# Two-layer transformer on one core: the softmax rescale moves to GpSimd, and the attention pipeline's offsets change

## The reference

```python
def _L0_attn_ref(x, Wq, Wk, Wv):            # H, R = 8, 64; d = 128
    Q = (x @ Wq.T).reshape(b, n, H, R)
    K = (x @ Wk.T).reshape(b, n, H, R)
    V = (x @ Wv.T).reshape(b, n, H, d)
    attn = jnp.einsum('bnhr,bmhr->bhnm', Q, K)
    attn = jax.nn.softmax(attn, axis=-1)
    return jnp.einsum('bhnm,bmhd->bnd', attn, V)
...
def _L0_ffn_ref(...):                        # 8 experts, top 1, capacity 80
    ...
    dispatch = jnp.einsum('nec,nd->ecd', sec_mask, tokens)
    h = jax.nn.gelu(jnp.einsum('ecd,edf->ecf', dispatch, w1) + b1[:, None, :])
    expert_out = jnp.einsum('ecf,efd->ecd', h, w2) + b2[:, None, :]
    return jnp.einsum('nec,ecd->nd', combine_weights, expert_out)
```

## Time and profile before

| | |
|---|---|
| time, median of 3 runs | 1496.58 us (1493.58 to 1497.97) |
| the profiled execution | 1496.05 us, of which the span 1494.3 us |
| first layer's attention (first copy of activations to the last result) | 31.28 to 421.00 us |
| busy over the whole span | PE 82%, DVE 86%, ACT 78%, POOL 53% |
| chain that ended last, by line | DVE L1024 17%, PE L1304 9%, PE L1317 7%, DVE L1010 6% |

### The profile page before, as it was taken

The page is one execution under the profiler, slowest core; times in us unless marked ns, Lnnn a source line. Parts: engine busy times, 40 slices in busy tenths (PEclk is TensorE's granted clock), DMA queues, the critical chain, the costliest instruction groups (busy, mean ns, idle before and its releaser), DMA issues.

```text
span 1494.3 us, 25209 instructions
## 1 busy us (share of the span) xinstructions
PE 1229.9 (82%) x6185; PEld 575.0 (38%) x6185; DVE 1280.2 (86%) x3505; ACT 1158.9 (78%) x1324; POOL 789.9 (53%) x1166
## 2 busy tenths in 40 slices
PE   2798687878864788899888988899888998899887
PEld 1476455555541233333333333333333333333333
DVE  5686687878866689999999999999999999999997
ACT  1566576767725689998899899998899998998960
POOL 2702100000000278878788777888788877887730
PEclk7899899999977799999999999999999999999998
DMA  5002200000000000000000000000000000000001
GB/s 183 13 1 34 16 1 0 0 0 0 0 1 18 7 19 26 19 18 21 26 23 18 18 28 25 18 18 18 28 25 18 18 28 25 18 18 18 28 25 32
DMA packets 38780, 31.58 MB, mean 21 GB/s; under 512 B 6150, under 2 KB 35609, under 8 KB 38738
## 3 DMA queue, kind: packets, MB, share of 16 engines
q1 hardware_dynamic: 37714, 29.76, 6.7%
q0 software_dynamic: 1024, 1.35, 1.0%
HBM read 29.10 MB, written 2.75 MB: 21 GB/s over the span
## 4 chain that ended last, share of the span: by engine, by line
DVE 30%; PE 26%; issue 9%; DVEq 3%; ACT 1%; POOL 0%; ACTq 0%
DVE arena L1024 17%; PE ps L1304 9%; PE ps L1317 7%; DVE arena L1010 6%; PE ps L1361 4%; PE ps L1381 2%; PE ps L1353 2%; DVE x L1067 2%; PE ps L1335 2%; DVE z L1050 2%; DVE spread L1076 1%; DVE nmax L1016 1%; DVEq L1023 1%; DVEq L1067 1%; ACT arena L1161 1%
## 5 line engine op out<-in xcount | busy, mean ns | idle before, releaser
L1024 DVE SCALAR_TENSOR_TENSOR arena<-arena,ps 128x512 f32<-128x512 f32 x1024 | 663.1, 679 | 65.9 <-PE ps L1317 65.7
L1161 ACT ACTIVATE arena<-arena,eps 128x4096 f32<-128x4096 f32 x128 | 474.3, 3709 | 38.6 <-POOL arena L1284 38.1
L1317 PE MATMUL ps<-spread,sel 128*128 128x512 f16 x1024 | 348.5, 386 | 118.4 <-DVE arena L1024 112.1
L1278 POOL TENSOR_SCALAR arena<-kT,negq 128x512 f32<-128x512 f32 x480 | 331.6, 701 | 196.5 <-DVE arena L1024 181.3
L1284 POOL TENSOR_SCALAR arena<-arena,q 128x512 f32<-128x512 f32 x480 | 351.8, 743 | 22.4
L1304 PE MATMUL ps<-arena,phi_cols 128*32 128x512 f32 x2048 | 276.4, 614 | 20.2 <-ACT arena L1161 20.2
L1317 PEld LDWEIGHTS ps<-spread,sel 128*128 128x128 f16 x1024 | 92.1, 97 | 513.0 <-DVE arena L1024 438.4
L1149 ACT ACTIVATE arena<-kT,q 128x512 f32 (+1 forms) x330 | 217.8, 715 | 3.0
L489 ACT ACTIVATE kT<-ps,region 128x512 f32<-128x512 f32 x128 | 88.2, 689 | 101.3 <-DVE region L559 97.7
L1270 POOL TENSOR_SCALAR negq<-q 128x256 f32<-128x256 f32 x4 | 3.5, 870 | 297.6 <-POOLq L762 297.6
L1010 DVE TENSOR_SCALAR arena<-kT,q 128x512 f32 (+1 forms) x214 | 141.9, 686 | 0.3 <-PEq L762 0.3
(11 more groups left out here) (196 smaller groups left out, 1794.9 us busy)
## 6 DMA issues: line engine op xcount, KB each, us to landing
wge<-in_e_wg SPq DMA_DIRECT2D x32, 256.0 KB, 2.7
w1e<-in_e_w SPq DMA_DIRECT2D x32, 128.0 KB, 2.1
w2e<-in_e_w SPq DMA_DIRECT2D x32, 128.0 KB, 2.1
w3e<-in_e_w SPq DMA_DIRECT2D x32, 128.0 KB, 2.1
region<-in_w SPq DMA_DIRECT2D x1, 2048.0 KB
out<-x SPq DMA_DIRECT2D x4, 256.0 KB, 2.7
region<-in_wqk SPq DMA_DIRECT2D x1, 512.0 KB, 4.6
region<-in_wv SPq DMA_DIRECT2D x1, 512.0 KB, 5.3
```

The lines of the kernel that those rows point to most:

```text
L1024: dve.scalar_tensor_tensor(feat[:, j, k, :], feat[:, j, k, :], 1.0, psB[:, k % BANKS, :], ALU.mult, ALU.mult, accum_out=sums[:, j, gg, c:c ...
L1161: act.activation(grp, grp, ACT.Sqrt, bias=eps[:]).then_inc(e_ready, 2)
L1278: pool.tensor_scalar(feat[:, j, QUADS * gg + c, :], kT[:, b * N:(b + 1) * N], HUGE, negq[:, b % 2, at - b * N // 2:at - b * N // 2 + 1], A ...
L1317: pe.matmul(psB[:, k % BANKS, :], sel[:, gg, c, :], spread[:, j, :], start=True, stop=True).then_inc(bc_done, 1)
```

## The change

The rescale of every step goes to GpSimd, so L567 on VectorE and L496 on ScalarE disappear, with the semaphore `act_p_ready`. The offsets change: queries and keys of the next head are projected in step 0 of a head instead of 1, their high parts made in step 1 instead of 2, their low parts in step 2 instead of 3. The transposes come 3 steps behind instead of 2, `pT_lo` 4 instead of 3, and the value products 5 instead of 4. The output of the batch before is taken at step 6 instead of 5, and the drain is one step longer. GpSimd's other work is now dealt out between the rescales: three scatters first and the other 13 one behind each rescale of batch 0, one part of the constants behind each rescale from step 16 of batch 0 on, and one gather behind each rescale of steps 2 to 17 of batch 1. GpSimd's list is written out for all 128 steps.

```diff
-        ON_ACT = (2,)
-        QK_AT, QK_HI, QK_LO = 1, 2, 3
-        LAG_T, LAG_LO, LAG_W = 2, 3, 4
+        QK_AT, QK_HI, QK_LO = 0, 1, 2
+        LAG_T, LAG_LO, LAG_W = 3, 4, 5
...
-
-        OUT_AT = 5
+        SCATTERS_FIRST, CONSTANTS_AT, GATHERS_AT = 3, 16, 2
+
+        OUT_AT = 6
         DRAIN = OUT_AT + 3
...
+            def rescale(n):
+                pool.wait_ge(rden_ready, n + 1)
+                pool.tensor_scalar(ex[:, n % 4, :], ex[:, n % 4, :], 1.0, rden[:, n % 4:n % 4 + 1],
+                                   ALU.mult, ALU.mult).then_inc(p_ready, 1)
+
+            pool.wait_ge(zeroed, 1)
+            for t in range(SCATTERS_FIRST):
+                scatter(t)
+            for b in range(B):
+                for s in range(STEPS):
+                    rescale(b * STEPS + s)
+                    if b == 0 and s + SCATTERS_FIRST < NT:
+                        scatter(s + SCATTERS_FIRST)
+                    if b == 0 and s >= CONSTANTS_AT:
+                        prepare_constants(pool, g, c2_made, c2_prep, s - CONSTANTS_AT)
+                    if b == 1 and 0 <= s - GATHERS_AT < NT:
+                        gather(s - GATHERS_AT)
             pool.wait_ge(gathered_in, 16 * NT)
...
-                    late = s - 1
-                    if late % TB in ON_ACT and runs(late, first, drain):
-                        act.wait_ge(rden_ready, b * STEPS + late + 1)
-                        act.activation(ex[:, late % 4, :], ex[:, late % 4, :], ACT.Copy,
-                                       scale=rden[:, late % 4:late % 4 + 1]).then_inc(act_p_ready, 1)
...
-                        if late % TB not in ON_ACT:
-                            dve.wait_ge(rden_ready, b * STEPS + late + 1)
-                            dve.tensor_scalar(ex[:, late % 4, :], ex[:, late % 4, :], rden[:, late % 4:late % 4 + 1], None,
-                                              ALU.mult).then_inc(p_ready, 1)
...
-                            pe.wait_ge(p_ready, b * (STEPS - sum(by_act)) + late + 1 - n)
+                        pe.wait_ge(p_ready, b * STEPS + late + 1)
```

More of the change, by code:

```diff
@@ L401, in first_layer @@
         qk_done, qk_kept = sem("qk_done"), sem("qk_kept")
-        k_lo_filled, act_p_ready = sem("k_lo_filled"), sem("act_p_ready")
+        k_lo_filled = sem("k_lo_filled")
         q_hi_kept, k_hi_kept, v_hi_kept, lo_kept = (sem("q_hi_kept"), sem("k_hi_kept"), sem("v_hi_kept"),
@@ L444, in _, with scatter @@
             pool.memset(zero, 0.0).then_inc(zeroed, 1)
-            for t in range(NT):
+            def scatter(t):
                 pool.indirect_dma_start(
@@ L449, in _, with gather @@
                     g.xn[:, t, :], None, bounds_check=SLOTS - 1, oob_is_err=False).then_inc(g.scattered, 16)
-            pool.wait_ge(zeroed, 1)
-            prepare_constants(pool, g, c2_made, c2_prep)
-            pool.wait_ge(eo_out, 16)
-            for t in range(NT):
+            def gather(t):
+                if t == 0:
+                    pool.wait_ge(eo_out, 16)
                 pool.indirect_dma_start(
@@ L668, in row @@
                     if runs(late, first, drain):
-                        by_act = [k % TB in ON_ACT for k in range(STEPS)]
-                        n = sum(by_act[:late % STEPS + 1]) - (sum(by_act) if late < 0 else 0)
-                        if late % TB in ON_ACT:
-                            pe.wait_ge(act_p_ready, b * sum(by_act) + n)
-                        else:
-                            pe.wait_ge(p_ready, b * (STEPS - sum(by_act)) + late + 1 - n)
+                        pe.wait_ge(p_ready, b * STEPS + late + 1)
                         if not first or late >= 2:
@@ L727, in _, with prepare_constants @@
             row(B, drain=True)
-def prepare_constants(pool, g, made, prep):
-    pool.memset(g.sel[:], 0.0).then_inc(made, 1)
-    pool.memset(g.mask_c, 1.0).then_inc(made, 1)
-    pool.memset(g.phi_cols[:], 0.0)
-    pool.memset(g.weT[:, D:DV], 0.0)
-    pool.memset(g.V2[:, :, D:DV], 1.0)
-    pool.memset(g.sumsT[:], 0.0)
-    pool.memset(g.exT[:], 0.0)
-    pool.memset(g.eps[:], EPS_RHO)
-    pool.memset(g.rho, -math.sqrt(EPS_RHO))
-    pool.wait_ge(made, 2)
-    v = g.sel[:].rearrange("p g c (h a) -> p g c h a", h=2)
-    for gg in range(GROUPS):
+def prepare_constants(pool, g, made, prep, part):
+    v = g.sel[:].rearrange("p g c (h a) -> p g c h a", h=2)
+    if part == 0:
+        pool.memset(g.sel[:], 0.0).then_inc(made, 1)
+    elif part == 1:
+        pool.memset(g.mask_c, 1.0).then_inc(made, 1)
+        pool.memset(g.phi_cols[:], 0.0)
+        pool.memset(g.weT[:, D:DV], 0.0)
+        pool.memset(g.V2[:, :, D:DV], 1.0)
+    elif part == 2:
+        pool.memset(g.sumsT[:], 0.0)
+        pool.memset(g.exT[:], 0.0)
+        pool.memset(g.eps[:], EPS_RHO)
+        pool.memset(g.rho, -math.sqrt(EPS_RHO))
+    elif part < 3 + GROUPS:
+        gg = part - 3
+        if gg == 0:
+            pool.wait_ge(made, 2)
         for half in range(2):
@@ L751, in prepare_constants @@
                 ins.then_inc(prep, 1)
-    pool.affine_select(out=g.mask_c, in_=g.mask_c, compare_op=ALU.is_ge, fill=0.0, base=-16,
-                       pattern=[[-32, QUADS]], channel_multiplier=1).then_inc(made, 1)
-    pool.wait_ge(made, 3)
-    pool.affine_select(out=g.mask_c, in_=g.mask_c, compare_op=ALU.is_ge, fill=0.0, base=31,
-                       pattern=[[32, QUADS]], channel_multiplier=-1).then_inc(made, 1)
+    elif part == 3 + GROUPS:
+        pool.affine_select(out=g.mask_c, in_=g.mask_c, compare_op=ALU.is_ge, fill=0.0, base=-16,
+                           pattern=[[-32, QUADS]], channel_multiplier=1).then_inc(made, 1)
+    elif part == 4 + GROUPS:
+        pool.wait_ge(made, 3)
+        pool.affine_select(out=g.mask_c, in_=g.mask_c, compare_op=ALU.is_ge, fill=0.0, base=31,
+                           pattern=[[32, QUADS]], channel_multiplier=-1).then_inc(made, 1)
 def second_route(nc, g, take):
```

## The result

The changed kernel took 1505.63 us, median of 4 runs (1502.41 to 1508.69), against 1495.47 for the kernel before beside it (1493.58 to 1497.97): ratio 1.0067, 95% interval 1.004 to 1.0093. I had forecast 1486 and a gain. It is slower.

The account below looks back on a forecast made before the run. The prediction took a chain through TensorE, VectorE and ScalarE in the first layer's attention as the bound; -5.5, -10.15, 2 x 1.85 and +1.3 summed to -10.65 us, giving 1486 us, range 1478 to 1501.

Parts of the forecast that it names:

- Walked on through the batch: Sum of the new order's changes over the seam and heads of a looped batch: +1.85 us each.
- The walk: Adding start-to-start edges along the first layer's chain through the engines; 9.84 us per head before, 9.83 in the new order.
- I expect both stalls to go: Spread indirect DMAs would remove the stalls in batches 0 and 1: 6.12 us and 12.0 us less.
- Rival (b): The burst of indirect DMAs does not make the stalls, so both stay: +7.9 us, 1504 us; chance 0.15.
- Cost nothing: The rescale on GpSimd, 701 ns, is hidden by two steps of cover; at most 1 us a step otherwise.
- Batch 0, -5.5: First batch: 8.3 us less from stall, held rescale and clock, against +1.1, +2.0 and about -0.3 elsewhere.
- Heads: Heads without value projections would take 9.83 us in the new order, those with two 11.34.
- For the seam the walk had +0.8: At a batch's start, the first scores of head 1 would come 0.8 us later.
- The drain, +1.3: At the end, half a head's value products ahead of the last transposes and the last GpSimd rescale: +1.3 us.
- the second layer, taken as 0: The layer after the changed attention, left alone by the change, got no term in the sum.

Follow-up runs that it names:

- filler_light: Changed kernel plus one-pass filler matmuls in the loop, ten at a batch's seam, six ahead of the transposes of steps 7 and 15; 1500.92 us, ratio 1.0124.
- before_again: The kernel before, unchanged, profiled again beside the experiments; 1480.41 us in its one run.
- e1_spread_only: Kernel before with only GpSimd's scatters, constants and gathers paced by step, rescale still on VectorE and ScalarE; 1482.52 us, ratio 1.0005.
- e2: Changed kernel with all offsets of before, keeping the rescale on GpSimd and the spread DMAs; 1475.93 us, ratio 0.9944 to the kernel before.
- filler_loop: Changed kernel plus one-pass fillers in batches 1 to 3: ten at seams, six in steps 3 to 15, four in steps 19 to 31; 1487.16 us, ratio 1.0031.
- after_again: The changed kernel, unchanged, timed again beside the kernel before; 1506.6 us, ratio 1.016.
- filler_all: Changed kernel plus one-pass fillers, ten at the loop's seams and six ahead of every head's step 3 transposes in all batches; 1495.12 us, ratio 1.0088.
- lag_only: Changed kernel with queries and keys projected and split in steps 1 to 3 as before, the longer lags kept; 1553.88 us, ratio 1.0484.
- qk_only: Changed kernel with the lags of before (2, 3, 4, output at 5), the earlier projection and split kept; 1551.01 us, ratio 1.0464.
- e3: Kernel before with the new offsets alone, rescale on VectorE and ScalarE, indirect DMAs in bursts; 1532.48 us, ratio 1.033.

## Why the prediction was wrong, point by point

**The step that failed first: "Walked on through the batch", +1.85 us per looped batch.** The walk took each edge at the duration that the trace of before has, nearly all of them at the full clock (0.99 in batch 2). It found that the new order moves TensorE's waits into fewer places and did not ask what the engine's clock does behind them. Batch 2 grew by 8.71 instead of 1.85. Fillers in these waits brought 5.6 of the 6.9 us of the difference back, at a clock of 1.00. Of the 1.3 left, some 0.8 stands in three filled heads (11.63, 11.61 and 10.97 instead of 11.34, 11.34 and 10.7), where the fillers came late. So the mechanism of the walk was right and its condition was not met. The clock is shown as the cause, by a kernel that does more work in less time and by heads of one kernel that differ by 1.65 us with the clock alone (`filler_light`). Why the clock falls behind one wait and not behind an equal one is not shown.

**The step that failed second: "I expect both stalls to go", -12.0 us in batch 1 and -6.1 in batch 0.** The stalls are absent from both profiles of the changed kernel. They are also absent from `before_again`, with the bursts unchanged, and `e1_spread_only`, which only deals the bursts out, gains nothing there. That the bursts suffice to make them is refuted, by three profiles with bursts and no stall; what made them in the first profile was not found, and no run beside the experiments had them to take away. Beside the result the change got back some 12 us of this kind (9.2 in batch 1 and 3.0 in batch 0, by the two profiles of before) and so looked like a loss of 10; where the kernel before has no stalls it is a loss of 1.6% (1.0146 to 1.0174), 23.7 us. Rival (b), 1504, gave nearly the measured time, but by another mechanism: the stalls went, and other losses took their place. In batch 1 the changed kernel's clock takes back about half of what its stall was worth: -12.0 plus 1.85 forecast, -4.74 measured.

**The rescale on GpSimd, "Cost nothing": right, and worth something.** 692 ns against the 701 expected. With the new lags the transposes wait for it once in the whole attention, 0.73 us in the drain. With the lags of before they wait 0.45 to 0.78 on 27 occasions, about once a head, and the batch is still no longer. It gains in batch 0, 6.6 us from `e1` to `e2`: the rescale that VectorE no longer has was held 3.90 us in `e1` and 4.45 in `before_again`, not 2.27. The Trainium skill ("GPSIMD Engine Reference", Key points) says that GpSimd shares its SBUF interfaces with VectorE, with contention in some of VectorE's modes. This agrees: the same instruction takes 0.49 without the memset beside it. In which mode it ran no run shows.

**Batch 0, -5.5: -6.21 measured.** The size is right, but its largest term was the stall. Against `before_again` it is only -3.1.

**Heads: right to 0.05 us where the clock is full.** 9.78 to 9.80 for 9.83, 11.31 for 11.34. For the seam the walk had +0.8 to the first scores of head 1: they stand 16.59 us behind the copy in batch 2 of `filler_loop` and 15.38 before, 1.2 more, of which about 0.3 are the late fillers of head 0.

**The drain, +1.3: right.** From the last row maximum to the last result it is 10.34 us (418.13 to 428.47) and was 9.11 (411.89 to 421.00), so +1.2. Batch 3 with the drain less batch 2 gives +0.8 (10.21 and 9.40), but in that the rest of the two batches stands too.

**A term that the sum did not have: the second layer, taken as 0.** It takes 1068.8 to 1076.3 us in the profiles, highest in both of the changed kernel (1075.6 and 1076.3) and in `filler_light`, with no change to it. Some 4 us of the 5.9 between `after_again` and `filler_all` lie in its first 55 us. Windows of 5 us at the same distance from the last result, 15 and 20 us behind it, of `after_again`, then of `filler_all`:

```profile
443.57:448.57 5.00, 5.00 (x25) 4.63 (x24) 2.20 (x12) 1.46 (x3) 0.00 (x0) 0.50 0.00 0
448.57:453.57 5.00, 5.00 (x18) 3.98 (x19) 1.48 (x6) 0.00 (x0) 0.00 (x0) 0.50 0.01 3
```

```profile
440.02:445.02 5.00, 5.00 (x39) 4.63 (x38) 2.19 (x12) 1.46 (x3) 0.00 (x0) 0.84 0.00 0
445.02:450.02 5.00, 5.00 (x16) 2.84 (x16) 2.22 (x7) 1.35 (x3) 0.00 (x0) 0.69 0.00 0
```

TensorE is full in both, with 25 matmuls in the first window of the one and 39 in that of the other: the one at the lower level throughout, the other for a part of the time at the upper (0.84 and 0.69). `e2_old_offsets` has the slow form too and `filler_all`, with the new offsets, the fast one, so the order in the first layer does not decide it; what does is open.

**Left open.** Why each half of the offsets alone costs 68 and 72 us is only half explained: for `lag_only` by clock and chain; for `qk_only` not, whose heads without value projections take 12.7 us at a clock of 0.84 in batch 2, with TensorE standing 2.80 for a remainder and 0.74 for a rescale in each. How the clock behaves was read only as levels behind waits. At the seams of `before_again` a wait of 3.09 in batch 1 was followed by scores of 0.79 and one of 3.08 in batch 2 by scores of 0.49, so the length of one wait alone does not tell.

## What to carry to other kernels

An order of instructions that leaves the chain's length unchanged can still cost: look where it gathers TensorE's idle time, read the granted clock in short windows behind these places, and price the matmuls there at both levels. A few one-pass matmuls into a free bank, placed in a wait that nothing shortens, are a cheap test of this and may be kept (4.5 us of 1483 at three seams here, and in the profiles only at seams where the clock had fallen); they must end before the wait does. And a stall that the profile of one run puts down to nothing on the core should be seen in a second profile before its removal is counted as a gain.

## What was not expected of the hardware

- The clock's fall moves: when two waits were filled, it came at the next one, which had been harmless (head 5, from 9.8 to 11.48 us). And one kernel has it at a wait in one batch and not at the same wait, equally long, in the next (2.29 and 2.30 us in `filler_light`).
- The kernel before took 1493.6 to 1498.0 us beside the result and 1477.9 to 1487.2 beside all experiments. 9.2 us of the difference between its two profiles lie in batch 1, 3.0 in batch 0, 3.8 in the second layer. The changed kernel took 1505.6 and 1506.6.
- One VectorE instruction of 0.49 us took 4.45 beside a GpSimd memset of 128x4096, longer than the memset's own 3.54. In other profiles it took 2.27 (the first of before), 3.90 (`e1`) and 5.76 (`e3`).
